# Attention output with key-value and key sums stationary in four column groups, query features moving

## The reference

```python
q_f = jax.nn.elu(jnp.einsum('bhnd,hdf->bhnf', q, proj)) + 1.0
k_f = jax.nn.elu(jnp.einsum('bhnd,hdf->bhnf', k, proj)) + 1.0
kv = jnp.einsum('bhnf,bhnd->bhfd', k_f, v)
attn = jnp.einsum('bhnf,bhfd->bhnd', q_f, kv)
k_sum = jnp.sum(k_f, axis=2)
z = 1.0 / (jnp.einsum('bhnf,bhf->bhn', q_f, k_sum) + EPS_ATTN)
attn = attn * z[..., None]
x = residual + attn @ w_out.T + b_out
```

## Time and profile before

| | |
|---|---|
| time of three runs | 753.7, 752.77, 752.85 us, median 752.85 |
| the profiled execution | 751.93 us, its span 750.2 us |
| PE busy over the span | 689.4 us, 92% |
| attention steps 1 to 6 | 88.8 to 197.4 us |
| from step 7 to `out_rows(7)` | 197.4 to 231.1 us |
| mean granted clock of PE | 0.953 of full |

### The profile page before, as it was taken

How to read it: one execution, slowest core, us unless ns; L and a number is a source line. 1 busy time by engine, 2 the same in 40 slices (tenths; PEclk the granted TensorE clock), 3 DMA queues, 4 the chain that set the end, 5 groups by cost and what they waited for, 6 DMA issues and landing times.

```text
span 750.2 us, 14597 instructions
## 1 busy us (share of the span) xinstructions
PE 689.4 (92%) x4607; PEld 610.2 (81%) x4608; DVE 339.4 (45%) x1006; ACT 294.2 (39%) x762; POOL 289.0 (39%) x324
## 2 busy tenths in 40 slices
PE   0887999999999999999999829999999999999994
PEld 0766888889888877888888629999999999999993
DVE  6584656665632545555444452333333333233330
ACT  0431656566532455354444403433334233332430
POOL 7012767676652533545350420322323232232321
PEclk9978999999859999999999959999999999999998
DMA  9514999800000496001100526221122122112210
GB/s 219 202 15 92 289 272 285 208 0 0 2 0 1 151 376 219 15 30 44 44 30 15 171 67 189 33 38 26 35 36 41 33 35 36 24 34 43 35 21 0
DMA packets 53221, 63.96 MB, mean 85 GB/s; under 512 B 6348, under 2 KB 48768, under 8 KB 53008
## 3 DMA queue, kind: packets, MB, share of 16 engines
q1 hardware_dynamic: 41264, 50.61, 23.8%
q0 software_dynamic: 8112, 9.04, 7.2%
q10 hardware_dynamic: 3808, 3.82, 1.6%
HBM read 31.01 MB, written 31.38 MB: 83 GB/s over the span
## 4 chain that ended last, share of the span: by engine, by line
PE 77%; DVE 8%; DMA 4%; issue 3%; POOL 3%; ACT 2%; SPq 0%; POOLq 0%; DVEq 0%; ACTq 0%
PE bank L1644 73%; DMA arena<-in_L_tok_Wa 2%; PE bank L2154 1%; DVE arena L997 1%; POOL routed_rows L780 1%; DMA h<-arena 1%; POOL small L545 1%; PE bank L1822 1%; DVE small L524 1%; POOL arena L729 1%; PE bank L1676 1%; DVE dense L537 1%; ACT arena L1533 1%; DVE arena L917 0%; DVE arena L920 0%
## 5 line engine op out<-in xcount | busy, mean ns | idle before, releaser
L1644 PE MATMUL bank<-arena,dense 128*128 (+2 forms) x1408 | 306.6, 389 | 1.1 <-ACT arena L1434 0.8
L1644 PEld LDWEIGHTS bank<-arena,dense 128*128 128x128 f32 (+1 forms) x1408 | 247.2, 193 | 36.7 <-ACT arena L1533 2.9
L822 POOL DMA_INDIRECT out_tokens<-dense,slot_ids x40 | 77.6, 1940 | 222.3 <-DVE dense L1360 214.5
L1614 ACT ACTIVATE dense<-bank,small 128x128 f32<-128x128 f32 x320 | 91.3, 369 | 182.9 <-PE bank L1644 182.9
L1644 PEld LDWEIGHTS bank<-dense 128*128 128x128 f32 x1280 | 150.1, 193 | 1.9
L1644 PE MATMUL bank<-dense 128*128 128x128 f32 x1280 | 150.2, 276 | 0.0
L1644 PE MATMUL bank<-dense,arena 128*128 128x256 f32 (+2 forms) x688 | 108.0, 359 | 1.1 <-ACT arena L1447 0.7
L1644 PEld LDWEIGHTS bank<-dense,arena 128*128 128x128 f32 (+2 forms) x688 | 83.9, 192 | 17.1 <-issue 4.5
L729 POOL TENSOR_TENSOR arena<-arena 128x512 f32<-128x512 f32 x64 | 80.3, 1279 | 42.0 <-ACT arena L1467 42.0
L1533 ACT ACTIVATE arena<-bank,small 128x256 f32<-128x256 f32 x128 | 53.7, 471 | 81.7 <-PE bank L1644 81.6
L1644 PE MATMUL bank<-arena 128*128 128x34 f32 (+7 forms) x756 | 81.7, 301 | 3.3 <-ACT arena L1533 1.9
(11 more groups left out here) (235 smaller groups left out, 561.4 us busy)
## 6 DMA issues: line engine op xcount, KB each, us to landing
routed_rows<-x SPq DMA_DIRECT2D x8, 2385.0 KB, 25.7
arena<-in_L_ffn_w SPq DMA_DIRECT2D x13, 1024.0 KB, 12.6
dense<-routed_rows SPq DMA_DIRECT2D x40, 132.5 KB, 2.1
arena<-in_L_ffn_w ACTq DMA_DIRECT2D x3, 1024.0 KB, 8.7
arena<-in_x SPq DMA_DIRECT2D x4, 512.0 KB, 6.9
arena<-in_L_attn_w SPq DMA_DIRECT2D x2, 1024.0 KB
out_tokens<-h SPq DMA_DIRECT2D x8, 256.0 KB, 2.2
h<-arena SPq DMA_DIRECT2D x13, 128.0 KB
```

The lines of the kernel that those rows point to most:

```text
L822: pool.indirect_dma_start(out=sums[:, :], out_offset=bass.IndirectOffsetOnAxis(ap=slot_ids[par][:, 0:1], axis=0), in_=y[par], in_offset=No ...
L1614: act.activation(hT[par][:, k, :], psUP[par][c][:, P * m:P * m + P], ACT.Silu, bias=b1now[par][:, k:k + 1]).then_inc(hT_sb, 1)
L1644: return pe.matmul(out, lhsT, rhs, start=start, stop=stop, **kw)
```

## The change

The attention output of an image is made in one call, with the roles of the operands exchanged. A pair's 32 key-value columns (`kv_st`) are stationary and the pair's query features of all 256 tokens move, and the output of pair m lands on the 32 partitions 32 (m % 4) of psX: eight matmuls with 128 rows, 32 columns and 256 moving columns, in four column groups. A second set of eight has the key sums stationary, each repeated 16 times (`ks_st`), and writes the denominators in the same layout to psT (for the last image to psL[1]). The output is then already transposed, feature by token.

ACT writes the two stationary tiles out of `kvbd` at the end of each step (`stationaries`, two copies of 256 columns) and moves the denominators out of the bank with EPS added, as a bias (`totals_out`, 512 columns, after bank 2). DVE's `attention_rows` becomes one call after `norm_tokens`: a reciprocal of all 512 columns of `dens` and one multiply of 512 columns out of psX into `attT`. The transposes `att_T` of PE and the copy `att_T` of ACT are gone. `key_values(g)` waits for `attention_rows(g-1)` as before. POOL gets one memset at the start (`eps`). No DMA is added, removed or moved. Semaphores `attT_ps` and `attT_sb` become `kv_sb` and `den_sb`.

```diff
--- before.py
+++ after.py
@@ -161,8 +161,10 @@
         catt = cut(arena, 2 * B * GROUP).rearrange("p (b a n) -> p b a n", a=2, b=B)
         c_qw = cut(arena, PAIRS * GROUP).rearrange("p (m n) -> p m n", m=PAIRS)
         c_den = cut(arena, 2 * B * 2).rearrange("p (a b h) -> p a b h", a=2, b=B)
-        att = [cut(arena, T * D).rearrange("p (t n) -> p t n", t=T) for _ in range(2)]
+        kv_st, ks_st = (cut(arena, PAIRS * GROUP).rearrange("p (m n) -> p m n", m=PAIRS) for _ in range(2))
+        dens = cut(arena, KD * IMG).rearrange("p (k n) -> p k n", k=KD)
         attT = [cut(arena, KD * IMG).rearrange("p (k n) -> p k n", k=KD) for _ in range(2)]
+        assert cut_at[0] <= ROWS * IMG
         at(ROWS * IMG)
         kf = [cut(arena, T * HEADS * FEAT).rearrange("p (q t c n) -> p q t c n", q=4, t=T, c=KD) for _ in range(2)]
         xn = [cut(arena, T * D).rearrange("p (t n) -> p t n", t=T) for _ in range(2)]
...
@@ -502,9 +507,9 @@
         psTotal = [bank[5][:, 2 * P:2 * P + 8], bank[5][:, 2 * P + 8:2 * P + 12]]
         psCQ = bank[5][:, 3 * P:3 * P + PAIRS]
-        def attended(g, j):
-
-            return psL[1] if j and isinstance(g, int) and g >= B - 2 else psX
+        def totals_bank(g):
+
+            return psL[1] if isinstance(g, int) and g == B - 1 else psT
         def relay(eng, b, j, done):
...
@@ -1028,15 +1034,12 @@
             token_stats(0, 0)
-            def attention_rows(g, par, j):
-
-                dve.wait_ge(attn_ps, T * g + j + 1)
-                src = attended(g, j)[:, 0:PAIRS * PW].rearrange("p (h d) -> p h d", h=HEADS)
-                d3 = den[:, j, :].rearrange("p (h o) -> p h o", o=1)
-                link(dve.tensor_scalar(d3, src[:, :, HD:VA], EPS_ATTN, None, ALU.add))
-                link(dve.reciprocal(den[:, j, :], den[:, j, :]))
-                dve.tensor_tensor(att[par][:, j, :].rearrange("p (h d) -> p h d", h=HEADS), src[:, :, 0:HD],
-                                  d3.to_broadcast([P, HEADS, HD]), ALU.mult).then_inc(att_ready, 1)
+            def attention_rows(g, par):
+
+                dve.wait_ge(den_sb, g + 1)
+                link(dve.reciprocal(dens[:, :, :], dens[:, :, :]))
+                dve.tensor_tensor(attT[par][:, :, :], psX[:, :].rearrange("p (k n) -> p k n", k=KD), dens[:, :, :],
+                                  ALU.mult).then_inc(att_ready, 1)
             norm_tokens(0, 0)
             dve.wait_ge(relaid[1], 16)
@@ -1072,12 +1075,10 @@
                                       ).then_inc(f_neg, 1)
                 for i in range(4):
                     negatives(i)
-                if not peeled or g >= 1:
-                    attention_rows(g - 1, 1 - par, 0)
                 if not peeled or g + 2 < B:
                     norm_tokens(g + 2, par)
                 if not peeled or g >= 1:
-                    attention_rows(g - 1, 1 - par, 1)
+                    attention_rows(g - 1, 1 - par)
                 if peeled and g == 0:
                     dve.wait_ge(relaid[3], 16 * T)
                 if not peeled or g + 3 < B:
@@ -1118,7 +1119,7 @@
             def turn(it):
                 attention_step(2 * it + 1, 1)
                 attention_step(2 * it + 2, 0)
-            chain.loop((B - 4) // 2, 10, turn)
+            chain.loop((B - 4) // 2, 4, turn)
             for g in range(B - 3, B):
                 attention_step(g, g % 2)
@@ -1135,8 +1136,7 @@
                     den4 = c_den[:, a, :, :].rearrange("p b (h o) -> p b h o", o=1)
                     dve.tensor_tensor(dst, halves[a][:, :, :, 0:HD], den4.to_broadcast([P, B, 2, HD]), ALU.mult
                                       ).then_inc(catt_ready, 1)
-            attention_rows(B - 1, 1, 0)
-            attention_rows(B - 1, 1, 1)
+            attention_rows(B - 1, 1)
             dve.wait_ge(x1_ready, 2)
             norm_x1(1, 1)
             dve.wait_ge(pads_stored, 16 * E)
@@ -1442,9 +1442,20 @@
                 act.wait_ge(k_ps, g + 1)
                 act.copy(kT[par][:, :, :], psL[0][:, :].rearrange("p (k n) -> p k n", k=KD)).then_inc(k_sb, 1)
-            def att_T(g, par):
-                act.wait_ge(attT_ps, g + 1)
-                act.copy(attT[par][:, :, :], psT[:, :].rearrange("p (k n) -> p k n", k=KD)).then_inc(attT_sb, 1)
+            def totals_out(g):
+                act.wait_ge(attn_ps, g + 1)
+                act.activation(dens[:, :, :], totals_bank(g)[:, :].rearrange("p (k n) -> p k n", k=KD), ACT.Identity,
+                               bias=eps).then_inc(den_sb, 1)
+
+            def stationaries(g):
+                act.wait_ge(kvbd_ready, g + 1)
+                if isinstance(g, int) and g == 0:
+                    act.wait_ge(c_done, 6)
+                after(act, attn_ps, g)
+                kv = kvbd[:, bass.ds(g, 1), :, :].rearrange("p o m (h d) -> p (o m) h d", h=2)
+                act.copy(kv_st.rearrange("p m (h d) -> p m h d", h=2), kv[:, :, :, 0:HD])
+                act.copy(ks_st.rearrange("p m (h d) -> p m h d", h=2),
+                         kv[:, :, :, HD:VA].to_broadcast([P, PAIRS, 2, HD])).then_inc(kv_sb, 1)
             tokens_T(0, 0)
             q_T(0, 0)
@@ -1470,6 +1481,8 @@
                 if not peeled or g + 1 < B:
                     q_T(g + 1, 1 - par)
                 bank_out(2)
+                if not peeled or g >= 1:
+                    totals_out(g - 1)
                 bank_out(3)
                 if not peeled or g + 1 < B:
                     k_T(g + 1, 1 - par)
@@ -1478,9 +1491,8 @@
                 if not peeled or g + 2 < B:
                     tokens_T(g + 2, par)
                 bank_out(6)
-                if not peeled or g >= 1:
-                    att_T(g - 1, 1 - par)
                 bank_out(7)
+                stationaries(g)
             attention_step(0, 0)
             with act.Fori(0, (B - 4) // 2) as it:
@@ -1535,9 +1547,8 @@
                     ins.then_inc(m_sb, 1)
             x1_T(0, 0)
-            hidden(0, 0, ACT.Gelu, b1T, gT, IMG, range(0, 2))
-            att_T(B - 1, 1)
-            hidden(0, 0, ACT.Gelu, b1T, gT, IMG, range(2, 4))
+            totals_out(B - 1)
+            hidden(0, 0, ACT.Gelu, b1T, gT, IMG, range(0, 4))
             x1_T(1, 1)
             act.wait_ge(cattT_ps, 1)
             act.copy(c_attT[:, :, :], psT[:, 0:KD * B].rearrange("p (k n) -> p k n", k=KD)
@@ -1754,7 +1765,7 @@
             def tokens_T(g, par):
                 pe.wait_ge(ln_ready, g + 1)
                 after(pe, xT_sb, g)
-                after(pe, attT_sb, g - 3)
+                after(pe, den_sb, g - 2)
                 for j in range(T):
                     for k in range(KD):
                         ins = pe.transpose(psT[:, k * IMG + j * P:k * IMG + j * P + P],
@@ -1812,19 +1823,8 @@
                         if c == KD - 1:
                             ins.then_inc(f_ps, 1)
-            def att_T(g, par):
-                pe.wait_ge(att_ready, T * g + T)
-                pe.wait_ge(xT_sb, g + 4 if not isinstance(g, int) or g + 4 <= B else B)
-                if isinstance(g, int) and g == B - 1:
-                    pe.wait_ge(x1T_sb, 1)
-                for j in range(T):
-                    for k in range(KD):
-                        ins = pe.transpose(psT[:, k * IMG + j * P:k * IMG + j * P + P],
-                                           att[par][:, j, k * P:k * P + P], ident)
-                ins.then_inc(attT_ps, 1)
-
             def out_rows(g, par):
-                pe.wait_ge(attT_sb, g + 1)
+                pe.wait_ge(att_ready, g + 1)
                 pe.wait_ge(k_sb, g + 3 if not isinstance(g, int) or g + 3 <= B else B)
                 for j in range(T):
                     for k in range(KD):
@@ -1838,33 +1838,28 @@
                 pe.wait_ge(f_sum, 8 * g + 4)
                 pe.wait_ge(v_sb, g + 1)
-                if not isinstance(g, int) or g >= 1:
-                    pe.wait_ge(att_ready, T * g - (1 if isinstance(g, int) and g == B - 1 else 0))
+                after(pe, att_ready, g)
                 for m in range(PAIRS):
                     for j in range(T):
                         ins = mm(psX[:, m * PW:(m + 1) * PW], kf[par][:, m % 4, j, m // 4, :],
                                  va[par][:, j, 2 * m:2 * m + 2, :].rearrange("p h d -> p (h d)"), j == 0, j == T - 1)
                 ins.then_inc(kv_ps, 1)
-            def attend(g, par, j):
-
-                if j == 0:
-                    pe.wait_ge(f_sum, 8 * g + 8)
-                    pe.wait_ge(kvbd_ready, g + 1)
-                elif attended(g, j) is psX:
-                    pe.wait_ge(att_ready, T * g + 1)
-                else:
-                    pe.wait_ge(att_ready, T * g)
-                    pe.wait_ge(v_sb, B)
-                for m in range(PAIRS):
-                    ins = mm(attended(g, j)[:, m * PW:(m + 1) * PW], qf[par][:, m % 4, m // 4, j * P:j * P + P],
-                             kvbd[:, bass.ds(g, 1), m, :].rearrange("p o n -> p (o n)"))
+            def attend(g, par):
+
```

(32 more changed lines are left out.)

## The result

The changed kernel takes 768.24 us in the median of four runs (767.62 to 769.91), the kernel before 752.81: a ratio of 1.0218, 95% interval 1.0189 to 1.0246, slower by 15.4 us where 6.5 were forecast. The profiled execution took 769.91 us with a span of 768.0, which is 17.8 us over the span before; the traces are compared on these.

What follows compares the result with a forecast made beforehand. PE was taken to bound the kernel. Six steps 105.4, plus falls 13.2, less 108.6, gave +10.0 us; with -3.5 at the end of attention, +6.5, so 758.4 profiled, 759.3 median; range 748 to 770, likeliest 754 to 766.

Steps and rivals of the forecast that it cites:

- the price of a fall: Time lost per clock fall in steps 1 to 6: 1.8 to 5.3 us, taken as 2.2, 13.2 us for six.
- the forecast itself: Likeliest case for the whole kernel: PE stalls and the clock falls in most steps, 754 to 766 us; chance 0.52.
- the third rival: Falls ahead of `key_values` at 3.5 to 5.3 us each, or slack on POOL and ACT lost: 767 to 777 us; chance 0.12.
- PE's own work: PE in a step: new `attend` takes 2.00 us, and work falls by 1.97 us, from 17.4 to 15.4.
- The reciprocal: DVE's reciprocal of 512 denominator columns in each image, priced from two short rows at 3.35 us.
- the rival of 801 us: Column groups of `attend` not side by side: 5.2 us more in each of eight calls, about 801 us; chance 0.03.
- The rival of the cheap reciprocal: PE stays the bound because the long reciprocal takes under 1.15 us: about 735 us; chance 0.08.
- The wait: PE idle 2.2 us ahead of `key_values` until DVE's multiply, giving steps of 17.6 us at full clock.
- The end of attention: Last stretch of attention, 197.4 to 231.1 in the kernel before: -3.5 us, with `key_values(7)` starting 1.6 us later.
- The clock: Steps 1 to 6: longer thin stretch, 5.7 us with idle time, makes the clock fall in nearly each; 2.2 us apiece.
- The first rival: PE stalls ahead of `key_values`, but the clock falls no more often than now: 749.7 us, faster; chance 0.25.

Runs made afterwards that it cites:

- x3: Changed kernel with DVE inverting only 32 of the 512 denominator columns, so part of the normalisation is left out: 744.2 us, ratio 0.9840 to the kernel before.
- x2: Changed kernel with PE doing the value matmuls of image g+1 an extra time ahead of `key_values(g)`, results overwritten: 754.0 us, ratio 0.9989 to the kernel before.
- x4: Kernel before with a useless 400-column reciprocal on DVE ahead of the second half's multiply, so `key_values` waits: 789.9 us, ratio 1.0460.
- x1: Changed kernel with PE's `values(g+1)` moved ahead of `key_values(g)`: 747.8 us, ratio 0.9905 to the kernel before; run again, 749.3 us, ratio 0.9927.
- x7: Changed kernel with `key_values` cut in two halves in steps 1 to 6 and `values(g+1)` between them: 763.2 us, ratio 1.0107 to the kernel before.
- x5: x1 with `key_values` halved in steps 1 to 6, `out_rows(g-1)` between, DVE's `v_rows` and `x1_rows` ahead of its `kvbd` adds: 741.2 us, ratio 0.9828.
- x6: Kernel before with `key_values` cut in two halves in steps 1 to 6 and `values(g+1)` between them: 755.2 us, ratio 1.0025.

## Why the prediction was wrong

The direction, the long reciprocal and PE's wait for it were right, and so was the number of falls, though not for the reason given. One term of the sum was mis-sized, the price of a fall, and with it the total: 768.2 us lies above the 754 to 766 of the forecast itself, and in the wide range of 748 to 770 only because that took in the lower part of the third rival.

- **PE's own work.** `attend` in 2.00 us: measured 1.86. The column groups run side by side, and the rival of 801 us was far off.
- **The reciprocal.** 3.35 us from two short rows: measured 3.352. By the Trainium skill (VectorE: DVE Perf Modes, First, the fixed hardware budget) the estimate was 1.0 us more, and the trace of the changed kernel does not agree with it. The rival of the cheap reciprocal falls with the 3.352 us; x3 shows what it would have been worth, 24 us against the changed kernel, and 744.2 us instead of the rival's 735, since the clock falls all the same.
- **The wait.** 2.2 us ahead of `key_values`: measured 1.8 to 2.0 in five steps, 2.4 in step 6. Steps of 17.6 us at full clock: x2 has them, 17.64 and 17.56, and the six steps of the changed kernel give 104.5 by their clock, where the prediction had 105.4.
- **The end of attention.** -3.5 us: measured 29.2 against 32.6, -3.4. `key_values(7)` began 8.8 us behind `key_features(7)` instead of 7.0, +1.8 for a forecast of +1.6, and ran at the low clock, as forecast.
- **The clock: the step that failed.** "I take it that the clock falls in nearly each of the six steps" was right, six of six, but that was in part luck: the reason was that idle time and `key_values` together make a longer thin stretch, and x3 had six falls too with at most 0.55 us of idle time. What failed is the price of a fall, put between 1.8 and 5.3 us: "I take 2.2, near the low end, since PE is idle through the first part and idle time does not stretch". The falls came inside `key_values` in every step, with PE busy throughout the low stretch, and the stretches were 6.8 or about 10 us long: 3.4 or 5 us each. The sum was 24.5 us (half of the 49 us of low time) where 13.2 were written. With 24.5 the same sum is 105.4 + 24.5 - 108.6 - 3.5 = 17.8, the difference of the spans; that it meets it to the tenth is chance, since the steps at full clock took 0.9 less than forecast and step 1 began 1.1 later. The third rival had this price, and 768.2 us is in its 767 to 777; it got a chance of 0.12.

That a wait ahead of `key_values` brings long falls is shown by x4, which has it alone. Why they are long is argued from the rows and was not tested by itself: a fall inside `key_values` makes what is left of it twice as long, and the earlier trace rows already had the case: in step 7 the clock stayed down through a whole `key_values` of 7 us. These rows should have priced it. That falls behind `key_values` are short (x1, x2, x3) and those inside it long (after, x4, x7) holds in nearly all steps of these runs. A long one does not need a long wait: x1 and x3 each have two of nearly 7 us, inside `key_values` too, after 0.9 us of idle time or less.

The first rival, no more falls than now, fails in the changed kernel, with six. What stays open is how many falls a schedule has: x1 and x2 have the same order of work up to the end of `key_values`, with `values` ahead of it, and have five and three (six in the second run of x1). No run here tells by what.

## What to carry to other kernels

A long reciprocal of a replicated denominator costs 6.25 ns a column on VectorE however many of the values are copies; where it stands on the path to a matmul that reuses a bank, price it from the slope of two short ones. Ahead of a stretch of thin matmuls (here 34 moving columns), a wait of TensorE can cost more than itself: here 2 us of it brought 6.8 to 10 us at half clock behind it, which cost 3.4 to 5. So price a fall by half of the low stretch that it can start, with the thin matmuls doubled. Then look for full-width work that can be moved into the wait (x1) and between the thin matmuls (x5); the second alone did little (x6, x7). With both, the kernel with the new form of `attend` is 1.7% faster than the kernel before (741.2 against 754.2 us); without them it is 2.2% slower. The kernel before was not tried with both.

## What the runs showed of the hardware that had not been expected

Adding 1.8 us of matmuls whose result is overwritten, to each of six steps, made the program 14 us shorter (x2). And waits of about the same length in the same place had unlike effects: in x7 two of six steps had the half clock for 14 us, which costs 7, and the last two, with waits of 1.82 and 2.40 us, not at all.
